# A ring of eight x tiles, fourteen result tiles, and a Pool counter in place of per-slot semaphores

## The chip, the cores and the metric

The kernel runs on one core of a Trainium2 chip. The metric is the device time of one execution in microseconds (us). The engines are TensorE (PE, with its weight loads shown as PEld), VectorE (DVE), ScalarE (ACT), GpSimd (POOL) and SyncE (SP); transfers run on 16 DMA engines that all queues share.

## What is computed

```python
# x: (128, 128, 1024) f32, itok_B_0_7: (128,) int in 0..7, L0_cond_weights: (8, 128, 128) f32
w = weights[subjects]                      # (128, 128, 128): a matrix for each b
out = jnp.einsum('bct,bcd->bdt', x, w)
return x + out
```

For each of 128 batch entries b, a 128 x 128 matrix, one of eight, is chosen by b's subject number, and its transpose is applied to x[b] of 128 x 1024; x itself is added. The kernel adds the identity to the eight matrices once, so that the residual costs nothing afterwards. 67.1 MB are read and 67.1 MB written, all in f32.

## The kernel before

**Tiles and pairs.** A tile is two batch entries, 64 tiles in all; a pair is two tiles, 32 pairs. x is loaded a pair at a time (2.1 MB, 128 partitions, two runs of 8 KB in each), and results are stored a pair at a time (2.1 MB, 16 KB in each partition). Entry a = 0 of a tile lies in the lower 64 partitions, a = 1 in the upper; the 128 rows of c are folded into R = 2 halves.

**Buffers.** `x_ring` has SLOTS = 10 tiles, five pairs; `results` has RESULTS = 6 pairs; `weight_ring` has a picked matrix for each slot of `x_ring`; `product` in PSUM holds PRODUCTS = 2 tiles.

**TensorE** (L233) makes 16 matmuls of 512 columns for a tile. Before each tile it waits until DVE and ACT have emptied the PSUM of two tiles earlier (`dve_copied`, `act_copied`), and before each pair until that pair's x is there. It waits on a semaphore of its slot: `x_first` for the first five pairs, `x_in` later. Its program writes ten tiles out, then a loop of ten tiles that runs five times, then four tiles (L244 to L250). Weights are guarded at a distance: DVE waits for `picked` three tiles ahead before it lets TensorE on (L185, L195).

**DVE and ACT** (L197, L219) copy the products out of PSUM, eight blocks of 32 x 1024 a tile, four or five of them by ACT. Before a pair they wait for the store that last used its place (`pair_out`).

**Pool** goes through the pairs (L137 to L156). For each it waits until the pair five earlier is multiplied, picks four matrices (two copies, L149, for each tile), and issues the load of x into the freed slots (L156). Every second pair it first loads four tiles' subject numbers into registers (L126). The first five loads are SP's (L108), the fifth after the first has landed.

**SP** then issues the 32 stores in order (L118). The store of pair p waits until the pair is copied, and until the load of pair p + 5 has landed:

```python
ahead = pair + PAIR_SLOTS
if ahead < PAIRS - 1:
    sp.wait_ge(x_in[ahead % PAIR_SLOTS], ahead // PAIR_SLOTS * DMA_INC)
```

So loads go ahead of stores; from pair 26 on a store waits for its copies alone.

Of the kernel before, what the change touches and what calls it, by code (L numbers as in the profile page):

```python
# [6 lines left out]
DMA_INC = 16  # L7
SLOTS = 10
PAIR = 2
LOADS_AHEAD = 4  # L10
PRODUCTS = 2
RESULTS = 6
# [3 lines left out]
def subject_residual_kernel(nc, x, subjects, weights, out):  # L16
# [19 lines left out]
    assert LAPS and SLOTS % PRODUCTS == 0 and REST % PRODUCTS == 0  # L36
    PAIRS, PAIR_SLOTS = TILES // PAIR, SLOTS // PAIR
    assert SLOTS % PAIR == 0 and REST % PAIR == 0 and LOADS_AHEAD < PAIR_SLOTS and PAIR * 2 * K == C
# [5 lines left out]
    ACT_BLOCKS = (4, 4, 5, 4, 5)  # L44

# [7 lines left out]
    with ExitStack() as ctx:  # L53
# [27 lines left out]

        picked = ctx.enter_context(nc.semaphore("picked"))
# [19 lines left out]
        def _(sp):  # L102
            sp.dma_start(weight_halves[:, :, :, :],
                         weights.rearrange("(i a) (h r) d -> (a h) i (r d)", a=2, r=R)).then_inc(weights_in, DMA_INC)
            for place in range(PAIR_SLOTS):
                if place >= LOADS_AHEAD:
                    sp.wait_ge(x_first[place - LOADS_AHEAD], DMA_INC)
                sp.dma_start(x_ring[:, place * PAIR:(place + 1) * PAIR, :, :], x_of_pair[place]).then_inc(x_first[place], DMA_INC)  # L108
            for pair in range(PAIRS):
                place = pair % RESULTS  # L110
                sp.wait_ge(act_copied, (pair + 1) * PAIR + PRODUCTS)
                sp.wait_ge(dve_copied, (pair + 1) * PAIR + PRODUCTS)


                ahead = pair + PAIR_SLOTS
                if ahead < PAIRS - 1:
                    sp.wait_ge(x_in[ahead % PAIR_SLOTS], ahead // PAIR_SLOTS * DMA_INC)
                sp.dma_start(out_of_pair[pair], results[:, place, :, :]).then_inc(pair_out[place], DMA_INC)  # L118
# [4 lines left out]
        def _(pool):  # L123
# [9 lines left out]
            for half in (LOW, HIGH):  # L133
                pool.affine_select(eye[half, :], eye[half, :], pattern=[[-1, H]], base=0, channel_multiplier=1,  # L134
                                   compare_op=mybir.AluOpType.not_equal, fill=1.0).then_inc(eye_made, 1)
            pool.wait_ge(clamped, 1)
            for pair in range(PAIRS):  # L137
# [8 lines left out]
                for j in range(PAIR):  # L146
                    slot = pair * PAIR % SLOTS + j
                    for a, half in enumerate((LOW, HIGH)):
                        done = pool.tensor_copy(weight_ring[half, slot, :, :],  # L149
                                                weight_bank[half, bass.ds(numbers[(pair % 2 * PAIR + j) * 2 + a], 1), :, :])  # L150
                    done.then_inc(picked, 1)
                if pair >= PAIR_SLOTS:

                    pool.wait_ge(picked, (pair + 1) * PAIR)
                    place = pair % PAIR_SLOTS
                    pool.dma_start(x_ring[:, place * PAIR:(place + 1) * PAIR, :, :], x_of_pair[pair]).then_inc(x_in[place], DMA_INC)  # L156

        @block.vector
        def _(dve):
# [13 lines left out]
            dve.sem_inc(dve_copied, 1)  # L173
# [11 lines left out]
            dve.wait_ge(picked, PRODUCTS)  # L185
            dve.sem_inc(dve_copied, PRODUCTS - 1)
            for tile in range(TILES):
# [4 lines left out]
                if tile + PRODUCTS < SLOTS:  # L192


                    dve.wait_ge(picked, tile + (PRODUCTS + 1))  # L195
# [27 lines left out]
        def _(pe):  # L223
            def multiply(tile, slot, landed, turns):
                pe.wait_ge(dve_copied, tile + 1)
                pe.wait_ge(act_copied, tile + 1)
                if slot % PAIR == 0:
                    pe.wait_ge(landed[slot // PAIR], turns)
# [14 lines left out]
            pe.wait_ge(picked, 1)  # L243
            for slot in range(SLOTS):  # L244
                multiply(slot, slot, x_first, DMA_INC)
            with pe.Fori(0, LAPS - 1) as lap:
                for slot in range(SLOTS):
                    multiply(lap * SLOTS + SLOTS + slot, slot, x_in, lap * DMA_INC + DMA_INC)
            for slot in range(REST):
                multiply(LAPS * SLOTS + slot, slot, x_in, DMA_INC * LAPS)  # L250
# [14 lines left out]
```

## Time and profile before

| | |
|---|---|
| Median of 3 runs | 324.1 us (323.81 to 324.17) |
| The profiled execution, its own time | 324.13 us |
| Its span, first to last instruction | 322.1 us |
| Busy: PE, DVE, ACT, POOL | 76%, 89%, 89%, 22% |
| DMA engines' mean rate | 419 GB/s |
| Moved, HBM read and written | 67.64 and 67.11 MB |

The span runs from the first instruction to the last; some 2 us of the device time lie around it. Busy shares are averages over the span. The DMA share is the mean busy share of the 16 engines: 1.0 means that none is idle, and it can read a little over 1 because packets overlap. A wait is put down to what ended it.

### The profile page before, as it was taken

Reading aid. Unit: us, or ns where it says so; the run is one execution under the profiler, and the core shown is the slowest. Engines: PE = TensorE matmul, PEld = TensorE weight load, DVE = VectorE, ACT = ScalarE, POOL = GpSimd, SP = SyncE. Lnnn points to the kernel's source line nnn. Section 1 sums busy time; section 2 is a strip of 40 time slices with the busy share of each in tenths; the row PEclk is TensorE's granted clock in tenths of the full one; section 3 lists DMA queues with packets and bytes.
Section 4 is the critical chain, followed back from the end, with each engine's and each line's share of the span. In section 5 each row is a group of like instructions: output and inputs, shape, how many; then the busy total and the mean of one; then the engine's idle time right before and its main releaser. Section 6 shows DMA issues by size and latency. Waiting matters only on the chain.

```text
span 322.1 us, 3197 instructions
## 1 busy us (share of the span) xinstructions
PE 246.1 (76%) x1036; PEld 103.6 (32%) x1036; DVE 286.9 (89%) x238; ACT 285.3 (89%) x283; POOL 71.2 (22%) x162
## 2 busy tenths in 40 slices
PE   8868878888887887789788888878977886885600
PEld 3323333333333333233333333333332333332200
DVE  4399999999999999999999999999999999796730
ACT  4299999999999999999999999999999999894730
POOL 1752222112222222221222222222222200000000
PEclk9999999999999999999999999999999999996955
DMA  7999999999999999999999999999999999999994
GB/s 280 423 423 421 428 441 409 431 424 428 429 426 435 425 432 419 426 441 418 432 435 427 417 430 432 426 422 437 419 429 434 426 430 422 440 426 431 429 429 208
DMA packets 13881, 134.85 MB, mean 419 GB/s; under 512 B 1056, under 2 KB 1584, under 8 KB 1584
## 3 DMA queue, kind: packets, MB, share of 16 engines
q1 hardware_dynamic: 6496, 78.12, 57.2%
q0 software_dynamic: 7344, 56.62, 41.8%
q8 instruction: 3, 0.05, 0.1%
q14 instruction: 6, 0.05, 0.0%
q10 hardware_dynamic: 32, 0.01, 0.0%
HBM read 67.64 MB, written 67.11 MB: 418 GB/s over the span
## 4 chain that ended last, share of the span: by engine, by line
DVE 39%; PE 27%; DMA 13%; ACT 9%; issue 7%; POOL 1%; ACTq 0%; POOLq 0%
DVE results L197 37%; PE product L233 27%; DMA x_ring<-x 11%; ACT results L219 9%; DMA weight_halves<-weights 1%; DVE weight_bank L167 1%; POOL weight_ring L149 1%; ACTq L53 0%; DVE weight_halves L162 0%; POOLq L149 0%; POOLq L126 0%; POOLq L142 0%
## 5 line engine op out<-in xcount | busy, mean ns | idle before, releaser
L219 ACT COPY results<-product 32x1024 f32<-32x1024 f32 x281 | 282.0, 1003 | 19.4 <-PE product L233 14.9
L197 DVE COPY results<-product 32x1024 f32<-32x1024 f32 x231 | 282.2, 1222 | 17.4 <-PE product L233 12.0
L233 PE MATMUL product<-x_ring,weight_ring 64*128 64x512 f32 x1024 | 238.8, 606 | 55.7 <-DVE results L197 39.9
L233 PEld LDWEIGHTS product<-x_ring,weight_ring 64*128 64x128 f32 x1024 | 100.6, 188 | 194.0 <-issue 107.1
L149 POOL COPY weight_ring<-weight_bank 64x256 f32 x128 | 50.9, 398 | 174.8 <-PE product L233 162.6
L156 POOL DMA_DIRECT2D x_ring<-x x27 | 19.4, 720 | 8.0 <-POOL weight_ring L149 8.0
L242 PE MATMUL product<-results 128*128 128x512 f32 x12 | 7.3, 772 | 1.5 <-DVE results L171 1.5
L203 ACT COPY weight_bank<-weight_halves 64x1024 f32<-64x1024 f32 x1 | 2.0, 2039 | 3.1 <-DVE weight_halves L162 3.1
L242 PEld LDWEIGHTS product<-results 128*128 128x128 f32 x12 | 3.0, 257 | 5.0 <-issue 3.5
L167 DVE COPY weight_bank<-weight_halves 64x1024 f32<-64x1024 f32 x3 | 3.2, 1074 | 0.1
L162 DVE TENSOR_TENSOR weight_halves<-weight_halves,eye 128x256 f32<-128x256 f32 x2 | 0.8, 423 | 2.2 <-DMA weight_halves<-weights 2.2
L203 ACT ACT_TABLE_LOAD x1 | 1.3, 1283 | 1.3 <-PEq L257 1.3
L171 DVE MEMSET results<- 128x512 f32 x1 | 0.5, 485 | 0.9 <-PEq L257 0.9
L175 DVE TENSOR_SCALAR subject_row<-subject_row 1x128 int32<-1x128 int32 x1 | 0.2, 215 | 1.0 <-DMA subject_row<-subjects 1.0
L134 POOL TENSOR_SCALAR_AFFINE_SELECT eye<-eye 64x64 f32<-64x64 f32 x2 | 0.5, 235 | 0.3 <-POOL eye L131 0.2
L131 POOL MEMSET eye<- 128x64 f32 x1 | 0.2, 152 | 0.3 <-POOLq L257 0.3
L257 POOL MEMSET const-float32-0.0<- 128x1 f32 x1 | 0.1, 93 | 0.3 <-issue 0.3
L257 POOL MEMSET const-float32-1.0<- 128x1 f32 x1 | 0.1, 93 | 0.0
L257 POOL MEMSET const-bfloat16-1.0<- 128x1 bf16 x1 | 0.1, 93 | 0.0
L257 POOL MEMSET const-uint8-127<- 128x1 uint8 x1 | 0.1, 93 | 0.0
## 6 DMA issues: line engine op xcount, KB each, us to landing
out<-results SPq DMA_DIRECT2D x32, 2048.0 KB, 12.1
x_ring<-x POOLq DMA_DIRECT2D x27, 2048.0 KB, 25.2
x_ring<-x SPq DMA_DIRECT2D x5, 2048.0 KB, 17.4
weight_halves<-weights SPq DMA_DIRECT2D x1, 512.0 KB, 4.1
subject_row<-subjects ACTq DMA_DIRECT2D x1, 8.0 KB, 1.7
```

What stands on the lines that cost most here:

```text
L134: pool.affine_select(eye[half, :], eye[half, :], pattern=[[-1, H]], base=0, channel_multiplier=1, compare_op=mybir.AluOpType.not_equal, fi ...
L149: done = pool.tensor_copy(weight_ring[half, slot, :, :], weight_bank[half, bass.ds(numbers[(pair % 2 * PAIR + j) * 2 + a], 1), :, :])
L156: pool.dma_start(x_ring[:, place * PAIR:(place + 1) * PAIR, :, :], x_of_pair[pair]).then_inc(x_in[place], DMA_INC)
L162: return dve.tensor_tensor(cells, cells, eye[:, :].rearrange("h (s k) -> h s k", s=1).broadcast_to((C, S // 2, H)), add)
L167: return dve.tensor_copy(weight_bank[half, subjects_of, :, :].rearrange("h i r (q k) -> h i r q k", q=Q), weight_halves[source, :, :, :].r ...
L171: dve.memset(results[:, RESULTS - 1, 0, 0:PSUM_BANK_COLS], 0.0).then_inc(zeroed, 1)
L197: last = dve.tensor_copy(target(tile, a, q), rows(tile, a, q))
L203: return act.copy(weight_bank[half, subjects_of, :, :].rearrange("h i r (q k) -> h i r q k", q=Q), weight_halves[source, :, :, :].rearrang ...
L219: last = act.copy(target(tile, a, q), rows(tile, a, q))
L233: last = pe.matmul(product[slot % PRODUCTS][a][:, cols], weight_ring[half, slot, r, :], x_ring[half, slot, r, cols], start=r == 0, stop=r ...
L242: pe.matmul(product[PRODUCTS - 1][0][:, 0:PSUM_BANK_COLS], zeros[:, 0:D], zeros, start=True, stop=True)
L257: nc = bacc.Bacc("TRN2", target_bir_lowering=False, num_devices=1)
```

## The change

The ring of x shrinks from ten tiles to eight (four pairs), and the results grow from six pairs to seven. Eight divides the 64 tiles, so TensorE's program is one loop of eight tiles that runs eight times. A new semaphore `arrived` is counted up by Pool, once for each pair in order, when the pair's weights are picked and its x has landed (`tell`). TensorE waits for this count before each pair, and SP for it before a store. The pair whose load a store waits for is now p + 2 + p // 8, so p + 2 for the first eight pairs and p + 5 for pairs 24 and 25; later pairs wait for none. The four first loads go out without a wait, and DVE no longer stands for the weights.

```diff
-SLOTS = 10
+SLOTS = 8
-LOADS_AHEAD = 4
-RESULTS = 6
+RESULTS = 7
...
+    def load_before(pair):
+        return pair + 2 + pair // 8
...
             for place in range(PAIR_SLOTS):
-                if place >= LOADS_AHEAD:
-                    sp.wait_ge(x_first[place - LOADS_AHEAD], DMA_INC)
                 sp.dma_start(x_ring[...], x_of_pair[place]).then_inc(x_first[place], DMA_INC)
...
-                ahead = pair + PAIR_SLOTS
-                if ahead < PAIRS - 1:
-                    sp.wait_ge(x_in[ahead % PAIR_SLOTS], ahead // PAIR_SLOTS * DMA_INC)
+                if load_before(pair) < PAIRS - 1:
+                    sp.wait_ge(arrived, load_before(pair) + 1)
...
+            def tell(pair):
+                lap, place = divmod(pair, PAIR_SLOTS)
+                pool.wait_ge(picked, (pair + 1) * PAIR)
+                if lap:
+                    pool.wait_ge(x_in[place], lap * DMA_INC)
+                else:
+                    pool.wait_ge(x_first[place], DMA_INC)
+                pool.sem_inc(arrived, 1)
...
+                pick(pair, numbers)
                 if pair >= PAIR_SLOTS:
-                    pool.wait_ge(picked, (pair + 1) * PAIR)
                     place = pair % PAIR_SLOTS
                     pool.dma_start(x_ring[...], x_of_pair[pair]).then_inc(x_in[place], DMA_INC)
+                if pair < 2:
+                    tell(pair)
+                elif pair >= PAIR_SLOTS:
+                    tell(pair - 2)
+            tell(PAIRS - 2)
+            tell(PAIRS - 1)
...
-            dve.sem_inc(dve_copied, 1)
+            dve.sem_inc(dve_copied, PRODUCTS)
...
-            dve.wait_ge(picked, PRODUCTS)
-            dve.sem_inc(dve_copied, PRODUCTS - 1)
...
-                if tile + PRODUCTS < SLOTS:
-                    dve.wait_ge(picked, tile + (PRODUCTS + 1))
...
                 if slot % PAIR == 0:
-                    pe.wait_ge(landed[slot // PAIR], turns)
+                    pe.wait_ge(arrived, pair + 1)
...
-            pe.wait_ge(picked, 1)
-            for slot in range(SLOTS):
-                multiply(slot, slot, x_first, DMA_INC)
-            with pe.Fori(0, LAPS - 1) as lap:
+            with pe.Fori(0, LAPS) as lap:
                 for slot in range(SLOTS):
-                    multiply(lap * SLOTS + SLOTS + slot, slot, x_in, lap * DMA_INC + DMA_INC)
-            for slot in range(REST):
-                multiply(LAPS * SLOTS + slot, slot, x_in, DMA_INC * LAPS)
+                    multiply(lap * SLOTS + slot, slot, lap * PAIR_SLOTS + slot // PAIR)
```

SP's program before, from the first loads on (a row is an instruction with what it waits for; x6 means six alike):

```order
L108 DMA x_ring<-x 128x2x2048 x4
L108 DMA x_ring<-x 128x2x2048 [waits x_first0]
L118 DMA out<-results 128x4096 [waits x_in0,dve_copied,act_copied]
L118 DMA out<-results 128x4096 [waits x_in1,dve_copied,act_copied]
L118 DMA out<-results 128x4096 [waits x_in2,dve_copied,act_copied]
L118 DMA out<-results 128x4096 [waits x_in3,dve_copied,act_copied]
```

SP's whole program now:

```order
L107 UNCONDITIONAL_BRANCH [waits barrier_Pool_Activation_PE_DVE_SP_release]
L109 DMA weight_halves<-weights 128x4x256
L112 DMA x_ring<-x 128x2x2048 x4
L119 DMA out<-results 128x4096 [waits arrived,dve_copied,act_copied] x26
L119 DMA out<-results 128x4096 [waits dve_copied,act_copied] x6
L57 UNCONDITIONAL_BRANCH [waits pair_out4,pair_out3,pair_out5,pair_out2,pair_out6,pair_out1,pair_out0]
```

The fifth load has left SP, and 26 stores wait for Pool's count where each waited for a load's own semaphore.

Pool's program before, the end of the picks of pair 5 and the start of pair 6 (ISA sets a register for the copy behind it):

```order
L149 ISA
L149 COPY weight_ring<-weight_bank 64x256
L156 DMA x_ring<-x 128x2x2048 [waits picked]
L126 TENSOR_LOAD subject_row
L149 ISA [waits multiplied]
```

Pool's program now, the end of the picks of pair 5 and the start of pair 6:

```order
L141 ISA
L141 COPY weight_ring<-weight_bank 64x256
L168 DMA x_ring<-x 128x2x2048
L127 TENSOR_LOAD subject_row [waits picked,x_first3]
L141 ISA [waits multiplied]
```

The wait before the load is gone, and the count of pair 3, with its wait for that pair's x, stands between the load of pair 5 and the register load of pair 6.

TensorE's program before, its start (the warm-up matmuls, then the first tile):

```order
L242 MATMUL product_0<-results 128x512 [waits zeroed]
L242 MATMUL product_0<-results 128x512 x5
L233 MATMUL product_0<-x_ring,weight_ring 128x512 [waits act_copied,x_first0,dve_copied,picked]
L233 MATMUL product_1<-x_ring,weight_ring 128x512
L233 MATMUL product_0<-x_ring,weight_ring 128x512
```

TensorE's program now, its start:

```order
L255 MATMUL product_0<-results 128x512 [waits zeroed]
L255 MATMUL product_0<-results 128x512 x5
L256 UNCONDITIONAL_BRANCH
L256 ISA
L241 ISA [waits act_copied,dve_copied]
L246 MATMUL product_0<-x_ring,weight_ring 128x512 [waits arrived]
L246 MATMUL product_1<-x_ring,weight_ring 128x512
```

The first matmul waited for `picked` and `x_first0`; it waits for Pool's count, inside the loop from the first tile on.

## Rows read from the trace of the kernel before

**Rows 1.** The page: busy share of the DMA engines, 40 equal slices.

```profile
DMA  7999999999999999999999999999999999999994
```

**Rows 2.** Windows: start:end, length, busy (x instructions) by engine, granted clock, DMA.

```profile
core 0: us, PE busy (x) PEld busy (x) DVE busy (x) ACT busy (x) POOL busy (x), PEclk, DMA share, GB/s
0.00:2.00 2.00, 0.54 (x1) 0.50 (x2) 0.48 (x1) 0.72 (x1) 0.82 (x7) 1.00 0.05 17
...
2.00:316.00 314.00, 245.56 (x1036) 103.06 (x1034) 286.43 (x237) 284.56 (x283) 70.37 (x155) 0.97 1.01 427
...
316.00:318.00 2.00, 0.00 (x0) 0.00 (x0) 0.00 (x0) 0.00 (x0) 0.00 (x0) 0.50 0.73 311
318.00:320.00 2.00, 0.00 (x0) 0.00 (x0) 0.00 (x0) 0.00 (x0) 0.00 (x0) 0.50 0.17 74
320.00:322.10 2.10, 0.00 (x0) 0.00 (x0) 0.00 (x0) 0.00 (x0) 0.00 (x0) 0.50 0.02 8
```

**Rows 3.** Timeline of Pool: start us, us, engine, line, operation, idle before and its end.

```profile
9.14 10.71 POOL L149 COPY weight_ring<-weight_bank 64x256 f32 x24 [7.47 <-DVE weight_bank L167]
20.16 0.83 POOL L156 DMA_DIRECT2D x_ring<-x  x1 [0.31 <-POOL weight_ring L149]
27.61 1.73 POOL L149 COPY weight_ring<-weight_bank 64x256 f32 x4 [6.62 <-PE product L233]
29.65 0.72 POOL L156 DMA_DIRECT2D x_ring<-x  x1 [0.31 <-POOL weight_ring L149]
...
254.19 0.72 POOL L156 DMA_DIRECT2D x_ring<-x  x1 [0.30 <-POOL weight_ring L149]
```

**Rows 4.** Waits: who waited for what, us in total, times, longest us.

```profile
SPq L117 <- DMA x_ring<-x: 259.5, 26, 24.7
...
PE product L233 <- DMA x_ring<-x: 3.9, 2, 3.0
```

**Rows 5.** The chain that ended last: start us, us, what.

```profile
0.74 4.07 DMA weight_halves<-weights
...
22.43 1.24 DVE results L197
23.72 3.73 PE product L233 x16
...
272.56 3.72 PE product L233 x16
293.60 6.29 PE product L233 x16
```

**Rows 6.** Timeline of TensorE's first two tiles, and of SP's DMA issues.

```profile
10.03 7.14 PE L233 MATMUL product<-x_ring,weight_ring 64*128 64x512 f32 x32 [1.29 <-POOL weight_ring L149]
...
1.24 8.93 SPq L108 DMA_DIRECT2D x_ring<-x  x5
...
9.80 0.37 SPq L108 DMA_DIRECT2D x_ring<-x  x1
34.98 0.36 SPq L118 DMA_DIRECT2D out<-results  x1
...
294.97 14.43 SPq L118 DMA_DIRECT2D out<-results  x2
...
309.07 0.33 SPq L118 DMA_DIRECT2D out<-results  x1
```

**Rows 7.** Line 126, Pool's register loads: ns min/median/max, first and last start us.

```profile
L126 POOLq TENSOR_LOAD <-subject_row x16: 562/1368/2338, 2.7 to 235.7; - x16
```

**Rows 8.** All loads of x, from issue to landing.

```profile
DMA to landing us min/median/max: 8.5/23.7/39.3
```

**Rows 9.** Windows again: loads alone, loads with stores, stores alone.

```profile
24.00:34.00 10.00, 8.67 (x40) 3.69 (x40) 9.80 (x9) 9.86 (x11) 2.31 (x5) 1.00 1.01 419
...
276.00:284.00 8.00, 6.42 (x32) 2.88 (x30) 7.60 (x7) 7.61 (x8) 0.00 (x0) 1.00 1.02 435
...
294.00:316.00 22.00, 9.30 (x32) 3.78 (x30) 9.46 (x8) 9.03 (x9) 0.00 (x0) 0.66 1.01 432
```

**Rows 10.** The page, DMA queues: one of instruction fetches; packets, MB, share.

```profile
q8 instruction: 3, 0.05, 0.1%
```

## What the change does to the time: the prediction

> **What bounds the kernel now.** I read the whole page first: the 16 DMA engines are busy in every slice but the first and the last two [rows 1]. The windows say it finer: a share of 1.01 and 427 GB/s on average from 2 to 316 us, then 0.73, 0.17 and 0.02 in the last three stretches, so a few engines finish late, while the compute engines, busy for 89% of the span, have nothing left to do there [rows 2]. And the Pool loads, which follow TensorE, are issued from 20.16 to 254.19 us, 26 intervals of 9.00 us [rows 3]. One pair moves 4.19 MB, which at 427 GB/s is 9.82 us. So copying (9.0 us a pair) outruns the transfers (9.8) and the transfers set the end. Third, the waits: SP waits 259.5 us for loads of x before it stores, while TensorE waits only 3.9 us for x in all, 3.0 of it once, before 272.56 [rows 4, 5]. Waits of the compute engines are therefore cheap; what counts is (a) how soon the DMA engines have work, (b) whether they ever run dry, (c) at what rate they run, (d) whether the last store is ready in time, (e) the uneven tail.
>
> **The sum's base.** The profiled execution took 324.13 us, 322.1 of it span; the median of the runs is 324.1, so the sum needs no shift. A measurement of this kernel can tell about 0.2% (0.65 us) from no change.
>
> **Part 1, the start.** SP issues the weights at 0.74 and the first x at 1.24 in both kernels [rows 5, 6]: no change. The first x has landed at 9.80, when SP is released for its fifth load [rows 6]; at 427 GB/s (4.9 us for 2.1 MB) loads 1 to 3 land at 14.7, 19.6 and 24.5. Now there are only these four, and three instructions later in Pool's program matter.
> TensorE no longer starts at Pool's second copy but at Pool's count, after four: copies take 0.45 us each (24 in 10.71 us from 9.14 [rows 3]), so 10.95 plus 0.1, against 10.03 [rows 6]: 1.0 us late. That is compute time, hidden by the 0.8 us a pair by which copying outruns the transfers.
> Pool then stands in the count of pair 1 until 14.7. Only then comes its load of the next subjects into registers, 0.6 to 2.3 us, 1.4 in the median [rows 7], no longer beside copies; then eight copies (a third of 10.71, 3.6 us), to 19.7. Pair 0's products are done at 10.03 + 7.14 + 1.0 = 18.2 [rows 6], so pair 4's picks run at once, 1.73 us, and load 4 goes out at 21.4, between 20.6 and 22.3 (before, load 5 at 20.16 [rows 3]).
> The SP loads feed the engines to about 24 (their landing less the way of the last bytes). From issue to first bytes I have only SP's row: issued at 0.74, and 17 GB/s over 0 to 2 us (34 KB) means a start near 1.9, so 1.2 us; the other end is the whole surplus of that load, 4.07 us less 1.2 us for its data, 2.9 us [rows 2, 5]. From 21.4, load 4 starts between 22.6 and 24.3: a hole of 0 to 0.3 us; I take 0.1. Farther out, if all went slowest, store 0 ends the hole: tile 1's copies end at 23.7 before [rows 5] and 24.7 now, so it starts at 25.9: at most 1.9 us.
> The Trainium skill (DMA: Bandwidth & Descriptors, Specifications) gives first bytes at about 1 us for GpSimd's path and 0.6 for SP's. The row shows 1.2 for SP, twice its figure; with GpSimd's doubled too, load 4 starts at 23.4 and there is no hole. Either way the sum stands within 0.1 us.
> Load 5: pair 1 is multiplied at 27.45 + 1.0; picks and issue as before (27.45 to 29.65, less the 0.3 us wait for the picks, which is gone) give 30.4 [rows 3, 5]. Load 4 and store 0 (4.9 us each) last until 33.9, and it starts by 33.3. From there each 9.0 us brings 9.8 us of work. **Term: +0.1; from 0 to +1.9.**
>
> **Part 2, the long middle.** The ring of x shrinks from five pairs to four. Load p+4 is issued about 2.8 us after pair p is multiplied (picks 1.73, gap 0.3, issue 0.72 [rows 3]) and TensorE wants it three pairs, 27 us, after that moment. Loads took 23.7 us in the median and up to 39.3 [rows 8], so TensorE will wait for x, often, late in the run, at a pace of 9.8 us a pair. Pool is now in front of it: the count of pair q stands between load q+2 and load q+3, and a late x(q) also holds up the picks and load q+3, and SP's store behind the same count. Is anything dry then? When x(q) lands, loads q+1 and q+2 (9.8 us of work) are queued, the count lets a store go, and load q+3 follows 2.8 us later. The margin is 7 us: never dry. Where the rule of the stores steps (pairs 8, 16, 24), a load passes without a store, 4.9 us, still inside it. Seven result places hold what the rule holds back: up to five waiting, one in flight, one being written. **Term: 0.**
>
> **Part 3, the rate.** Loads alone run at 419 GB/s (24 to 34 us), loads with stores at 435, stores alone at 432 [rows 9]. Before, the first store goes out at 34.98 [rows 6]; now at about 24.8, as soon as it is copied, its count (load 2) being there. That takes 10.2 us from the slow rate to the fast one: 10.2 x 16/435 = 0.4 us. The mean of 427 lies half way between 419 and 435, so before some half of the time goes by at the slow rate; each pair's cycle keeps such a stretch (a store of 4.9 us against 9.8), so I count the start only. Bounds: all of it at 435 where 427 was had, 314 x 8/435 = -5.8 us; loads never beside stores, 67.1 MB at 419 and 67.1 at 432, 315.5 us for 314: +1.5. Nearest is the start's own row. **Term: -0.4; I carry -1.5 (a quarter of the slow time gone) to +0.8.**
>
> **Part 4, instructions and the tail.** TensorE's program falls from 24 written-out tiles to 8. Instruction fetches take 0.1% of 16 engines' span on one queue [rows 10], some 5 us of one engine's time. If the lost fetches all sat on the engine that ends last, the end moves by up to about 3 us; spread evenly, by 0.2. TensorE waited for none of it. **Term: -0.1; from -3 to 0.** The added Pool instructions are waits and counts, and its picks and issues fill only 2.8 of each 9.0 us [rows 3].
> The last windows hold about 1.8 us of work for all engines in 6.1 us of time [rows 2]: about 4 us is imbalance. The skill's same page (Latency and other measured facts) says two DMA engines are usually slower beside GpSimd's queue, as a guess at its rings. No row here names an engine. By it one more Pool load (28 for 27) would add 4/27, 0.15 us.
>
> **Part 5, the end.** Let x(30) land at time 0. Then stores 25 to 28 are let go together, 29 to 31 follow, and load 31 is in flight: 5.0 + 7 x 4.9 = 39.3 us of transfers. The last pair needs 15.5 us from its first matmul to the last store's issue (293.60 to 309.07, with one TensorE tile at 6.29 instead of 3.73 [rows 5, 6]), and that store alone some 7.8 us (4.9 plus the 2.9 above). So x(31) may land as late as +16.0. Sharing evenly with one store it lands at +9.9; with two store bytes for each of its own (runs of 16 KB against 8 KB) at +14.7. Hidden, with 1.3 to 6 us to spare. **Term: 0.**
>
> **Sum.** 324.13 + 0.1 + 0 - 0.4 - 0.1 + 0 = **323.7**.
>
> **Rivals.**
> *Faster: the transfers gain rate or the tail evens out.* For it: the early stores are no longer held, and fetches shrink. Against: each pair keeps its stretch of loads alone. Were a quarter of those stretches gone (some 40 of 157 us, x 16/435 = 1.5, in place of the 0.4), the sum is 322.6.
> *Slower: the engines run dry at 24 us*, because load 4 now stands behind the count of pair 1 and Pool's path is slow to start. It decides where load 4's issue and the way to its first byte together pass 24.0: 2.6 us after an issue at 21.4. Price up to 1.9: 323.6 + 1.9 = 325.5. Against it: SP's 1.2 us.
> *Slower at the end:* x(31) later than +16 costs one for one. A load that takes the longest landing seen, 39.3 us, from its issue near -12 lands at +27: +11, 335. For it: four stores start at once against one load. Against: that load before had three loads ahead of it, this one has two.
> *It doesn't do what it says:* the early stores are held as before (SP behind the counts), and nothing moves: 324.1.
>
> **How the numbers follow.** Forecast 0.45, faster rival 0.24, dry start 0.16, late end 0.05, nothing moves 0.10. The range leaves out half of the late end and the outer parts of the others: **321.9 to 325.9**. Around the forecast itself lies 323.1 to 324.4, which gives a third of it to faster (under 323.45), almost none to slower. Faster 0.36, same 0.40, slower 0.24.
>
> **What would show it.** First store issued at 24 to 26 us; the window 24 to 34 near 435 instead of 419; TensorE starts near 11; Pool's first load near 21.4; 28 Pool loads; TensorE's waits for x grow from 3.9 to well over 10 us with the span unchanged; DMA share 1.0 to about 316 us; last store issued between 304 and 312. Wrong if a DMA window before 316 us falls under 0.95, if the last store goes out when the engines are already emptying, or if the share of the last 6 us changes its shape by over 1 us.

## The result and the profile after

The changed kernel takes 325.24 us in the median of 13 runs (324.30 to 326.43), the kernel before 324.04 (323.81 to 324.17): a ratio of 1.0044, interval 1.0032 to 1.0056. It is 1.2 us (0.4%) slower, and the interval leaves no doubt of the direction; 0.4 us faster was forecast. Its 13 runs spread over 2.1 us, the 13 of before over 0.4.

The profiled execution took 325.93 us, 323.8 of it span (before: 324.13 and 322.1), so it is one of the longer ones, and its profile shows the loss larger than a typical run has it. The page's DMA lines, in 40 slices:

```profile
DMA  7999999999999999999999999999999999999995
GB/s 287 423 410 425 316 433 430 419 437 419 438 418 431 436 427 420 436 420 430 435 419 432 428 422 437 422 423 433 424 428 423 438 429 415 437 426 432 431 429 235
```

The busy digits are those of before but for the last [rows 1]. The GB/s line shows what they hide: the fifth slice, 32 to 40 us, moved 316 GB/s, where all others between the first and the last moved 410 to 439. Windows of the changed kernel (columns as in [rows 2]):

```profile
core 0: us, PE busy (x) PEld busy (x) DVE busy (x) ACT busy (x) POOL busy (x), PEclk, DMA share, GB/s
23.00:29.00 6.00, 4.82 (x24) 1.98 (x22) 5.92 (x6) 5.28 (x6) 0.00 (x0) 1.00 1.00 390
34.00:39.00 5.00, 3.98 (x18) 1.46 (x16) 4.86 (x5) 4.93 (x6) 0.00 (x0) 1.00 0.92 272
23.00:39.00 16.00, 13.34 (x60) 5.13 (x56) 15.65 (x14) 15.14 (x16) 2.25 (x5) 1.00 0.99 367
60.00:316.00 256.00, 200.37 (x856) 82.12 (x852) 239.55 (x197) 239.66 (x239) 51.77 (x115) 0.97 1.01 428
316.00:318.00 2.00, 0.00 (x0) 0.00 (x0) 0.00 (x0) 0.00 (x0) 0.00 (x0) 0.50 1.01 434
318.00:320.00 2.00, 0.00 (x0) 0.00 (x0) 0.00 (x0) 0.00 (x0) 0.00 (x0) 0.50 0.82 352
320.00:323.80 3.80, 0.00 (x0) 0.00 (x0) 0.00 (x0) 0.00 (x0) 0.00 (x0) 0.50 0.11 47
```

Before, from the same view:

```profile
34.00:39.00 5.00, 4.32 (x22) 1.85 (x20) 4.88 (x5) 4.93 (x6) 2.21 (x5) 1.00 1.03 428
23.00:39.00 16.00, 13.28 (x58) 5.81 (x60) 15.65 (x14) 15.77 (x17) 4.52 (x10) 1.00 1.02 423
60.00:316.00 256.00, 197.64 (x847) 83.25 (x843) 236.96 (x194) 237.00 (x237) 50.74 (x110) 0.97 1.01 428
```

From 60 us to 316 both kernels move 428 GB/s: the long middle costs nothing. The loss lies ahead of it: 367 GB/s from 23 to 39 us for 423, with 390 in its first six microseconds and 272 from 34 to 39, where the kernel before had 428. The **share** there reads 1.00 and 0.92, so the share alone would not have found the hole: from 35 to 38 us Pool's queue has 117 packets (0.96 MB) at a share of 96.6% of the 16 engines' time, where the kernel before has 153 (1.25 MB) at 100.8%. A packet took longer, and an engine counts as busy meanwhile. The missing bytes, 56 GB/s x 16 us, are 2.1 us at 427. The last windows give some of it back: the 16 engines end closer together (352 GB/s from 318 to 320 us, against 74 in [rows 2]), and the span grows by 1.7 us only.

What stood where, in Pool's timeline, TensorE's, SP's, the chain, and two windows with the granted clock:

```profile
15.60 3.53 POOL L141 COPY weight_ring<-weight_bank 64x256 f32 x8 [2.68 <-DMA x_ring<-x]
20.04 1.74 POOL L141 COPY weight_ring<-weight_bank 64x256 f32 x4 [0.91 <-PE product L246]
21.72 0.83 POOL L168 DMA_DIRECT2D x_ring<-x  x1
30.30 1.73 POOL L141 COPY weight_ring<-weight_bank 64x256 f32 x4 [7.75 <-PE product L246]
31.98 0.72 POOL L168 DMA_DIRECT2D x_ring<-x  x1
...
11.03 8.83 PE L246 MATMUL product<-x_ring,weight_ring 64*128 64x512 f32 x32 [2.70 <-POOLq L153]
...
26.43 17.79 SPq L119 DMA_DIRECT2D out<-results  x3
301.52 9.07 SPq L119 DMA_DIRECT2D out<-results  x2
...
11.03 5.42 PE product L246 x16
...
11.00:17.00 6.00, 5.97 (x20) 2.66 (x22) 0.53 (x1) 0.53 (x1) 2.86 (x8) 0.72 1.00 419
17.00:20.00 3.00, 2.86 (x14) 0.97 (x10) 2.97 (x3) 2.96 (x4) 1.93 (x5) 1.00 1.03 429
```

TensorE idled 2.70 us between the warm-up and the first tile, waiting for Pool's count, and then took 5.42 us for that tile (3.73 before is the usual one [rows 5]). The granted clock had fallen: 0.72 on average from 11 to 17 us (0.50 from 12 to 13, the lower of its two levels, 1.2 GHz), and 1.00 from 17 to 20. Load 4 went out at 21.72, load 5 at 31.98, store 0 at 26.43. Of the three stores in the row from 26.43 on, the second was issued at 35.16; its bytes began only after 39 us, so from 34 to 39 load 5 alone was moving bytes.

TensorE's wait for Pool's count, and the instruction fetches of the page:

```profile
PE product L246 <- POOLq L153: 8.6, 4, 2.8
...
q8 instruction: 1, 0.02, 0.0%
```

TensorE waits for Pool's count 8.6 us in all, the 2.70 before the first tile among them; it waited 3.9 for x before [rows 4].

### The profile page after: what moved, and what is told of

Its sections match the earlier page's. It is cut to its first block, busy times and chain, and to the rows that moved or that the text cites. A ratio compares the mean times of both kernels' runs of the same rounds, so it can differ in the third digit from the quotient of the medians.

```text
span 323.8 us, 3264 instructions
## 1 busy us (share of the span) xinstructions
PE 248.0 (77%) x1036; PEld 101.8 (31%) x1036; DVE 286.9 (89%) x238; ACT 285.2 (88%) x283; POOL 70.3 (22%) x163
## 4 chain that ended last, share of the span: by engine, by line
DMA 46%; DVE 28%; PE 17%; issue 3%; POOL 1%; DVEq 0%; POOLq 0%
DMA x_ring<-x 45%; DVE results L210 26%; PE product L246 17%; POOL weight_ring L141 1%; DMA weight_halves<-weights 1%; DVE weight_bank L186 1%; DVEq L57 0%; DVE weight_halves L181 0%; POOLq L127 0%; POOLq L141 0%; POOLq L153 0%; POOLq L161 0%
## 5 line engine op out<-in xcount | busy, mean ns | idle before, releaser
L232 ACT COPY results<-product 32x1024 f32<-32x1024 f32 x281 | 281.9, 1003 | 19.9 <-PE product L246 16.1
L246 PEld LDWEIGHTS product<-x_ring,weight_ring 64*128 64x128 f32 x1024 | 98.9, 190 | 197.9 <-issue 131.1
L168 POOL DMA_DIRECT2D x_ring<-x x28 | 20.2, 720 | 0.0
```

Of the source, the lines that this page charges most:

```text
L232: last = act.copy(target(tile, a, q), rows(tile, a, q))
L246: last = pe.matmul(product[slot % PRODUCTS][a][:, cols], weight_ring[half, slot, r, :], x_ring[half, slot, r, cols], start=r == 0, stop=r ...
```

## The experiments

Theory 1: the DMA engines get too little work at the start. Why a transfer that is alone in flight then moves fewer bytes I first put down to Pool's path, later to its being alone. Theory 2: four first loads are too few, whatever comes next. Theory 3: Pool's count costs a little with every pair. A table of all, ahead of the single runs; GB/s are from the windows of the profiled execution, the ratio is to the kernel before on the same chip, whose median was 323.84 to 324.04 us.

| kernel | us | ratio, 95% interval | 23 to 39 us | 39 to 60 us | 60 to 316 us |
|---|---|---|---|---|---|
| before | 324.0 | | 423 | 430 | 428 |
| changed | 325.24 | 1.0044 (1.0032, 1.0056) | 367 | 424 | 428 |
| changed, loads 4, 5 by SP | 324.52 | 1.0022 (1.0011, 1.0033) | 424 | 426 | 429 |
| before, ring 8 | 327.18 | 1.0105 (1.0090, 1.0120) | 345 | 415 | 428 |
| changed, 8 warm-ups | 324.86 | 1.0029 (1.0019, 1.0039) | 403 | 428 | 429 |
| changed, count 1 later | 325.14 | 1.0033 (1.0015, 1.0052) | 400 | 427 | 429 |
| before, new rule | 324.18 | 1.0003 (0.9994, 1.0012) | 424 | 428 | 428 |
| before, count | 325.70 | 1.0067 (1.0048, 1.0086) | 411 | 400 | 428 |
| changed, all three repairs | 324.36 | 1.0017 (1.0009, 1.0026) | 423 | 425 | 428 |
| changed, first loads by Pool | 325.12, one run | | 392 | 433 | 428 |
| changed, SP's loads at Pool's hour | 324.91 | 1.0036 (1.0022, 1.0050) | 422 | 429 | 428 |
| before, count and rule | 323.91 | 1.0003 (0.9994, 1.0012) | 426 | 429 | 428 |
| changed, 1 warm-up | 327.14 | 1.0099 (1.0080, 1.0118) | 372 | 411 | 429 |
| before, ring 8, new rule | 324.63 | 1.0015 (1.0006, 1.0024) | 426 | 427 | 428 |
| as SP's at Pool's hour, 8 warm-ups | 324.61 | 1.0019 (1.0010, 1.0028) | 418 | 426 | 429 |

### SP issues loads 4 and 5

```diff
+                if pair < 2:
+                    sp.wait_ge(multiplied, (pair + 1) * PAIR)
+                    sp.dma_start(x_ring[...], x_of_pair[PAIR_SLOTS + pair]).then_inc(x_second[pair], DMA_INC)
                 sp.wait_ge(act_copied, (pair + 1) * PAIR + PRODUCTS)
```

> The changed kernel, with loads 4 and 5 of x issued by SP (waiting for pairs 0 and 1 to be multiplied) instead of Pool. The changed kernel moves only 367 GB/s from 23 to 39 us where the kernel before moves 423; that is 2.1 us of work. Theory 1 (the start runs short because Pool's path is slow to deliver when nothing else is queued): SP can issue load 4 at about 20 and load 5 at 28.8, and its path brings bytes 1.2 us later, so 23 to 39 us comes back to 415 or more and the time to 323.6 to 324.2 us. Theory 2 (four loads at the start are too few, whoever issues the next): the stretch stays below 390 and the time at 325. Theory 3 (the count in front of TensorE and SP costs a little in every pair): the time stays at 325 though the stretch recovers.

```profile
23.00:39.00 16.00, 12.62 (x58) 4.99 (x56) 15.65 (x14) 15.25 (x16) 3.14 (x9) 1.00 1.02 424
...
316.00:318.00 2.00, 0.00 (x0) 0.00 (x0) 0.00 (x0) 0.00 (x0) 0.00 (x0) 0.50 0.75 320
```

The hole is gone (424), and so is its mark on the tail: 320 GB/s from 316 to 318 us, near the 311 of before. The median falls by 0.7 us (the intervals of the two ratios just touch), but stays 0.5 above the kernel before, and above the 323.6 to 324.2 that I expected. SP issued at 18.2 and 28.4 us, 3.5 earlier than Pool, and in this profile the first tile ran on the high clock, so this run alone tells neither path from hour nor the clock's part.

### The ring alone, on the kernel before

```diff
-SLOTS = 10
+SLOTS = 8
-LOADS_AHEAD = 4
+LOADS_AHEAD = 3
-RESULTS = 6
+RESULTS = 7
...
-                if place >= LOADS_AHEAD:
-                    sp.wait_ge(x_first[place - LOADS_AHEAD], DMA_INC)
```

> The kernel before with a ring of eight tiles, seven pairs of results and four first loads without a wait, and nothing else: TensorE waits on the loads' own semaphores, the store of pair p waits for load p + 4. Theory 1 and 2 (the short start): store 0 is held until load 4 has landed, about 30 us, so between 24 and 33 us load 4 is alone and the stretch 23 to 39 us is at least as slow as in the changed kernel, 340 to 370 GB/s; the time is 325 to 327. Theory 3 (the count is to blame): without it the time is the old 324.

```profile
23.00:39.00 16.00, 13.10 (x58) 5.78 (x60) 15.65 (x14) 15.77 (x17) 4.34 (x10) 1.00 0.89 345
```

327.18 us (four runs), the slowest of all, without any count. So the count isn't needed for a loss at the start; whether it costs something with every pair, this run can't tell. SP holds store 0 for load 4, and load 5 goes out at 29.8 us too, so that the engines have next to nothing for two microseconds, and then a store alone:

```profile
28.00:30.00 2.00, 2.00 (x10) 1.04 (x11) 1.99 (x2) 1.98 (x3) 1.55 (x5) 1.00 0.36 147
30.00:35.00 5.00, 3.93 (x20) 1.65 (x18) 4.93 (x5) 4.93 (x6) 0.53 (x1) 1.00 0.88 315
...
29.89 0.36 SPq L116 DMA_DIRECT2D out<-results  x1
```

From 28 to 30 us 147 GB/s are moved, at a share of 0.36, and from 30 to 35, the store alone until load 5's bytes come, 315, at a share of 0.88. This transfer is SP's: a lone one can be slow on SP's queue too.

### More warm-up, and less

```diff
-WARM_UP = 6
+WARM_UP = 8
```

> The changed kernel with eight warm-up matmuls instead of six, so that TensorE doesn't stand idle for 2.7 us before the first tile. Its first tile took 5.42 us instead of 3.73, which makes loads 4 and 5 and stores 0 and 1 late by up to 1.7 us. Theory 1: with the first tile at 3.7 us, load 5 goes out at about 30.3 instead of 31.98, and 23 to 39 us gains half or more of the 2.1 us: 324.2 to 324.7 us. Theory 3: no change, 325.2.

```profile
10.97 7.14 PE L246 MATMUL product<-x_ring,weight_ring 64*128 64x512 f32 x32 [0.71 <-POOLq L153]
23.00:39.00 16.00, 12.62 (x58) 5.00 (x56) 15.65 (x14) 15.27 (x16) 3.81 (x10) 1.00 1.01 403
```

The first two tiles take 7.14 us instead of 8.83, and the stretch comes to 403. Of 1.2 us lost 0.4 come back, less than I expected; the intervals against the kernel before (1.0019 to 1.0039, 1.0032 to 1.0056) overlap, so this gain alone is not shown. With one warm-up the other way:

```diff
-WARM_UP = 6
+WARM_UP = 1
```

> The changed kernel with one warm-up matmul instead of six, so that TensorE's clock is low for its first tiles: the opposite of the run with eight. Theory 1: the first two tiles take up to 7.2 us each, loads 4 and 5 go out 2 to 5 us later, the stretch 23 to 39 us falls below 350, and the time rises to 326 to 328 us. If the start has slack for that, the time stays at 325.2.

```profile
10.97 6.55 PE product L246 x16
23.00:39.00 16.00, 13.49 (x62) 5.53 (x60) 15.72 (x14) 15.13 (x16) 2.85 (x6) 1.00 0.96 372
39.00:60.00 21.00, 16.96 (x76) 6.92 (x74) 20.52 (x18) 20.69 (x22) 6.54 (x15) 1.00 1.00 411
```

The first tile takes 6.55 us after 7.4 us of idling and the time is 327.14. This is the clearest dose: one number for TensorE's warm-up, changed in a kernel that the transfers bound, makes it 1.9 us slower (four runs; the two intervals lie apart). In the profiles the first two tiles end at 20.9 us instead of 19.9. The stretch itself didn't fall below 350, as I had expected (372); the rest of the loss is in the next one (411 for 424).

### Pool's second count, later

```diff
-                if pair < 2:
-                    tell(pair)
+                if pair == 0:
+                    tell(0)
+                elif pair == PAIR_SLOTS - 1:
+                    tell(1)
```

> The changed kernel, but Pool counts pair 1 only after it has picked for pairs 2 and 3, so that it no longer stands in that count until 14.8 us with the picks behind it. Theory 1: load 4 is then bound by pair 0 being multiplied (19.9) and goes out at 21.7 as before, since TensorE's late first tile and not Pool's picks sets it: no change, 325.2, within 0.3. If Pool's standing in the count is what makes load 4 late, it goes out a microsecond earlier and the time falls by 0.5 or more.

No change in the time, as expected (325.14, interval 1.0015 to 1.0052, a wide one), though load 4 went out at 20.3 us in the profile, not at 21.7, and the stretch ran at 400. Its profile had the first tile at 3.73 us after 1.86 us of idling, with the same six warm-ups: whether the first tile finds the high clock varies. So the 400 goes with the clock as much as with the edit; eight warm-ups alone gave 403.

```profile
11.32 7.14 PE L248 MATMUL product<-x_ring,weight_ring 64*128 64x512 f32 x32 [1.86 <-POOLq L153]
```

### The new rule for stores, alone

```diff
-                ahead = pair + PAIR_SLOTS
-                if ahead < PAIRS - 1:
+                ahead = pair + 2 + pair // 8
+                if ahead < PAIR_SLOTS:
+                    sp.wait_ge(x_first[ahead], DMA_INC)
+                elif ahead < PAIRS - 1:
                     sp.wait_ge(x_in[...], ...)
```

> The kernel before with the new rule for stores alone: the store of pair p waits for the load of pair p + 2 + p // 8, on the loads' own semaphores; ring of ten tiles, six pairs of results, five first loads. The first store then goes out at about 23.8 us instead of 34.98. My prediction's step on the rate: 10 us more of loads beside stores, at 435 instead of 419 GB/s, gives 0.4 us back: 323.6. The opposite reading (what is mixed early is missing from the mix later, since loads and stores are fixed amounts, and the runs after the change swing more): 324.0 or above, and the windows from 39 us on no faster than before.

```profile
23.00:39.00 16.00, 13.22 (x58) 5.82 (x60) 15.65 (x14) 15.77 (x17) 4.43 (x10) 1.00 1.02 424
39.00:60.00 21.00, 17.05 (x76) 7.00 (x74) 20.52 (x18) 20.64 (x21) 4.74 (x11) 1.00 1.01 428
60.00:150.00 90.00, 74.26 (x324) 31.04 (x322) 88.15 (x73) 88.39 (x89) 22.92 (x50) 1.00 1.01 429
150.00:270.00 120.00, 95.71 (x410) 41.04 (x408) 113.44 (x93) 113.33 (x114) 27.50 (x60) 0.99 1.01 427
```

324.18 us: no gain. The first store goes out at 23.8 instead of 34.98, and the stretch moves 424 GB/s where it moved 423; the later windows are at 427 to 429. My 0.4 us for the early mix was not there.

### Pool's count alone

```diff
-                    sp.wait_ge(x_in[ahead % PAIR_SLOTS], ahead // PAIR_SLOTS * DMA_INC)
+                    sp.wait_ge(arrived, ahead + 1)
...
-                    pe.wait_ge(landed[slot // PAIR], turns)
+                    pe.wait_ge(arrived, pair + 1)
```

with `tell` in Pool's program as in the change, on the ring of ten.

> The kernel before with Pool's count alone: TensorE and SP wait on it instead of the loads' own semaphores (ring of ten tiles, six pairs of results, old rule, five first loads). Theory 1 (four first loads with nothing behind them): with five, the stretch 23 to 39 us stays at 420 or more and the time at 324.0. Theory 3 (the count costs): up to 325, with no hole in that stretch.

```profile
23.00:39.00 16.00, 12.73 (x58) 5.34 (x56) 15.65 (x14) 15.25 (x16) 4.56 (x10) 1.00 1.00 411
39.00:60.00 21.00, 17.40 (x77) 7.02 (x73) 20.52 (x18) 20.70 (x21) 5.27 (x12) 1.00 1.00 400
```

Neither expectation held: the time is 325.70 (six runs), and the hole is there, but later: from 42 to 45 us, with SP's queue holding nearly all the bytes, 287 GB/s are moved, and from 39 to 60 only 400. The sixth load goes out at 25.8 instead of 20.16 us. A part of that is the count of pair 1, in which Pool stands until 15.56 us, so that its picks end at 22.7 instead of 19.9; for the 3.1 us from there to the issue this trace names no cause. Store 0 waits, now through Pool, until 38.4. From 60 us on it is 428. So the count does cost, but only at the start, through what it makes late.

### All three repairs

The edits of the first run, of the eight warm-ups and of the later count, together:

```diff
-WARM_UP = 6
+WARM_UP = 8
+SP_LOADS = 2
...
-                if pair < 2:
-                    tell(pair)
+                if pair == 0:
+                    tell(0)
+                elif pair == PAIR_SLOTS - 1:
+                    tell(1)
```

> The changed kernel with three repairs: loads 4 and 5 by SP, eight warm-up matmuls, pair 1 counted after the picks for pairs 2 and 3. Theory 1: the start is whole already with SP's loads (324.5 us, 424 GB/s in 23 to 39 us), so the other two add under 0.3 us: 324.2 to 324.6. If what remains of the loss beside the kernel before also comes from the start, it goes to 324.0 or below.

324.36 us, as expected: no better than SP's loads alone within the intervals, and still slower than the kernel before (1.0009 to 1.0026). By the medians the repairs of the start give back 0.9 of the 1.2 us; where the last 0.3 lie is not shown.

### Pool issues the first four loads too

```diff
-            for place in range(PAIR_SLOTS):
-                sp.dma_start(x_ring[...], x_of_pair[place]).then_inc(x_first[place], DMA_INC)
...
+            for place in range(PAIR_SLOTS):
+                pool.dma_start(x_ring[...], x_of_pair[place]).then_inc(x_first[place], DMA_INC)
             pool.memset(eye[:, :], 0.0).then_inc(eye_zero, 1)
```

> The changed kernel with the first four loads of x issued by Pool instead of SP, so that Pool's path is seen with nothing queued before it. Theory 1: in SP's hands the engines run at 423 GB/s from 4 us on; with Pool's, the first microseconds of the first load show the same stretched packets as loads 4 and 5 do in the changed kernel (its 34 to 39 us ran at 272 GB/s), and the first x lands 1 to 3 us later than 9.8. If Pool's path delivers as fast as SP's once started, only the start moves by under a microsecond and 4 to 23 us runs at 423.

```profile
4.00:23.00 19.00, 15.10 (x56) 6.32 (x56) 11.66 (x12) 9.73 (x9) 9.50 (x25) 1.00 1.02 425
23.00:39.00 16.00, 12.60 (x56) 4.88 (x54) 15.65 (x14) 15.13 (x16) 3.36 (x8) 1.00 1.00 392
```

From rest, Pool's path moves 425 GB/s from 4 to 23 us, like SP's. Its first microseconds are not slow; that part of theory 1 falls. The hole stays where it was (392). It is one run, and its time can't be judged.

### SP's loads at Pool's hour, with six and with eight warm-ups

Against the run in which SP issues loads 4 and 5:

```diff
+                    sp.wait_ge(picked, (PAIR_SLOTS + pair + 1) * PAIR)
-                    sp.wait_ge(multiplied, (pair + 1) * PAIR)
```

> The changed kernel with loads 4 and 5 by SP, but no earlier than Pool would issue them: SP waits until Pool has picked for pairs 4 and 5. It tells the path from the hour. SP's loads at 18.2 and 28.4 us had cured the hole (424 GB/s from 23 to 39 us, 324.5 us), Pool's stood at 21.7 and 32.0 (367 GB/s, 325.2 us). If the hour decides (theory 1 in its new form: a transfer that is alone in flight runs slowly, whoever issued it), the stretch stays at 365 to 395 and the time at 325.0 to 325.4. If Pool's path decides, the stretch goes to 415 or more and the time to 324.5.

With six warm-ups the profile had 422 GB/s from 23 to 39 us, SP's loads at 20.8 and 30.2 us, and the first tile on the high clock; the median of five runs is 324.91, between the two expectations and no better than the warm kernel with Pool's loads; the profiled execution was the fastest of the five (324.30). So, with the clock settled:

```diff
-WARM_UP = 6
+WARM_UP = 8
```

> Path against hour once more, with TensorE's first tile surely on the high clock: eight warm-up matmuls, and SP issues loads 4 and 5, but not before Pool has picked for their pairs (20.8 and 30.2 us). The twin with Pool's loads at the same hours gave 403 GB/s from 23 to 39 us and 324.86 us; with six warm-ups and SP's late loads the profile had 422 GB/s. If the path decides: 420 or more and 324.2 to 324.5 us. If the hour decides: about 403 and 324.8.

```profile
33.00:39.00 6.00, 4.61 (x20) 1.97 (x22) 5.84 (x6) 5.92 (x7) 1.46 (x4) 1.00 1.01 412
34.00:38.00 4.00, 3.21 (x16) 1.16 (x12) 3.89 (x4) 3.94 (x5) 0.56 (x2) 1.00 0.99 406
```
```profile
33.00:39.00 6.00, 4.74 (x22) 2.04 (x24) 5.84 (x6) 5.92 (x7) 1.57 (x5) 1.00 0.99 373
34.00:38.00 4.00, 3.13 (x18) 1.13 (x14) 3.89 (x4) 3.94 (x5) 0.67 (x2) 1.00 0.99 354
```

The first fence is SP's late load (issued at 30.4 us), the second Pool's at the same hour (30.2) with the same warm-up: 412 against 373 GB/s. These stretches hold the end of store 0 and the start of store 1 too; from 34 to 37 us, where next to nothing but load 5 moves, it is 412 against 347. The other profiles agree: SP's load 5 moved 410 to 412 in three kernels, Pool's 270 to 347 in four (the changed kernel, eight warm-ups, the later count, first loads by Pool). In the profiles the path decides; in the times it can't be told (324.61 and 324.86, intervals 1.0010 to 1.0028 and 1.0019 to 1.0039). The expected 420 or more was 418, and the time stayed above the 324.2 to 324.5 expected.

That a load is Pool's and alone is not enough, though. The kernel before has such a load at the same hour, the sixth, issued at 29.65 [rows 3]; so has the changed kernel, load 4, from 24 to 28 us:

```profile
34.00:38.00 4.00, 3.32 (x18) 1.40 (x16) 3.89 (x4) 3.94 (x5) 1.51 (x4) 1.00 1.02 420
```

The sixth load of the kernel before moved 420 GB/s, load 4 of the changed kernel 393, and 418 in the kernel with eight warm-ups. What tells these from load 5 (279 over the same 34 to 38 us) no run was made to find. The profiles hint at a head start: over 34 to 37 us, Pool's load issued at 29.65 moved 421, those issued at 30.22, 30.57, 31.09 and 31.98 moved 347, 341, 336 and 270. A rival stands untested beside it: DVE copies for 15.65 of the 16 us from 23 on, and for 11.66 of 19 in the stretch from 4 to 23 us where Pool's path moved 425; no run took DVE's copies away from a late load.

### The count and the rule, on the ring of ten

```diff
-                ahead = pair + PAIR_SLOTS
+                ahead = pair + 2 + pair // 8
                 if ahead < PAIRS - 1:
                     sp.wait_ge(arrived, ahead + 1)
```

> The kernel before (ring of ten, six pairs of results, five first loads) with Pool's count and the new rule for stores. The count alone gave 325.7 us: Pool's sixth load went out at 25.8 instead of 20.2 and the first store at 38.4, and from 39 to 60 us only 400 GB/s were moved. With the new rule the first store goes out at 25, beside two loads. Theory 1: no transfer is alone then, 23 to 60 us runs at 423 or more, and the time is 324.0 to 324.4. If the count itself costs in every pair, the time stays above 325.

```profile
23.00:39.00 16.00, 12.75 (x58) 5.25 (x56) 15.65 (x14) 15.18 (x17) 4.43 (x10) 1.00 1.01 426
39.00:60.00 21.00, 17.48 (x78) 7.10 (x74) 20.52 (x18) 20.65 (x21) 5.35 (x12) 1.00 1.01 429
60.00:316.00 256.00, 196.92 (x848) 81.35 (x848) 238.08 (x195) 237.85 (x238) 49.22 (x110) 0.98 1.01 428
```

323.91 us against 323.84: the whole loss of the count, 1.7 us, is gone as soon as the stores are let go early, though Pool's sixth load is still at 25.9 us. Stores fill the gap that late loads leave. The windows from 60 us on (428) and this time are what rules out theory 3.

### The ring and the rule, without the count

```diff
-SLOTS = 10
+SLOTS = 8
-LOADS_AHEAD = 4
+LOADS_AHEAD = 3
-RESULTS = 6
+RESULTS = 7
...
-                if place >= LOADS_AHEAD:
-                    sp.wait_ge(x_first[place - LOADS_AHEAD], DMA_INC)
...
-                ahead = pair + PAIR_SLOTS
+                ahead = pair + 2 + pair // 8
+                if ahead < PAIR_SLOTS:
+                    sp.wait_ge(x_first[ahead], DMA_INC)
...
```

> The corner that is missing between three parts of the change: ring of eight tiles, seven pairs of results and the new rule for stores, but the loads' own semaphores instead of Pool's count. The kernel before is 324.0, with the new rule 324.2, with the count 325.7, with both 323.9; with the ring of eight alone 327.2, with all three (the changed kernel) 325.2. If four first loads are enough as long as nothing else is late (TensorE starts at 10.1 on a high clock, Pool's load 4 goes out at 19.6 and load 5 at 29.7, store 0 at 23.8), the stretch 23 to 39 us is at 415 or more and the time 324.0 to 324.5: then the change's loss needs the ring and the count together. If four first loads are too few by themselves, the stretch is at 400 or less and the time 324.8 or more.

```profile
23.00:39.00 16.00, 13.23 (x58) 5.81 (x60) 15.65 (x14) 15.77 (x17) 4.46 (x10) 1.00 1.02 426
60.00:316.00 256.00, 197.81 (x848) 83.50 (x844) 237.00 (x194) 236.82 (x237) 53.01 (x115) 0.97 1.01 428
316.00:318.00 2.00, 0.00 (x0) 0.00 (x0) 0.00 (x0) 0.00 (x0) 0.00 (x0) 0.50 0.73 311
```

No hole at all (426), yet 324.63 us, in runs from 324.42 to 324.73. Its spans are 322.3 us in the median, 322.1 for the kernel before in the same rounds; the other 0.4 us lie outside the span. What they are I didn't find. Beside the ring of eight alone it is 2.6 us faster: the rule that gains nothing on the ring of ten is what makes the short ring nearly harmless.

**Together.** By parts, in us: ring of ten 324.0; with rule 324.2; with count 325.7; with both 323.9. Ring of eight 327.2; with rule 324.6; with both 325.2. With the rule, in ratios to the kernel before: count 1.0003, ring 1.0015, both 1.0044; the two together cost more than the sum. (The ring with the count and without the rule was not run.) Theory 1 stands in this form: with stores flowing early the count costs nothing on the ring of ten, and the short ring 0.6 us; with both, loads 4 and 5 are late **and** there are only four loads to live on until then. Theory 2 fails as it was put, since SP's earlier loads, or no count, fill the stretch from the same four. In every kernel the windows from 60 us on are the same, 428 or 429, and theory 3 is out.

## Why the prediction was wrong

**Base and bound.** Right: the transfers set the end, at 428 or 429 GB/s from 60 us to 316 in all 15 kernels.

**Part 1, the start: the step that failed.** The sum had +0.1 us, up to +1.9 in a rival; the experiments give most of the loss to this part (0.9 of 1.2 us come back with the three repairs). Three steps in it were wrong. First, I moved TensorE's first two tiles by the 1.0 us of Pool's count and kept their length of 7.14 us. They took 8.83 in the profile, because the idling before them grew to 2.7 us and the granted clock fell to its lower level. So store 0 went out at 26.43 instead of 24.8, and load 5 at 31.98 instead of 30.4; load 4 was near, 21.72 for 21.4. Second, I asked when each transfer's first byte comes, and took it to run at the full rate from there. Load 5, alone from 34 to 39 us, moved 272 GB/s: at 428 it would have moved the same bytes 1.8 us sooner. Load 4 cost less, with 390 GB/s from 23 to 29 us. Third, I had a store's bytes start 1.2 us after its issue, from SP's first load; store 0, issued at 26.43, moved none before 29 us, which left load 4 alone until then.

The Trainium skill (DMA: Bandwidth & Descriptors, Bandwidth) has smaller transfers slower: it lists 341 GB/s for 1 MB loaded through GpSimd and 425 for 16 MB. The Trainium skill (DMA: Bandwidth & Descriptors, Anatomy of one DMA — SWDGE (gpsimd) path) puts a fixed 2.0 us on each such transfer, beside its bytes at 436 GB/s. By these two figures a load of 2.1 MB alone takes 6.8 us, 308 GB/s (an estimate from that page). That section of the Trainium skill gives most of the 2 us to the confirmation after the last byte, which would not slow a stretch in the middle of a load. Load 5's 272 is nearer to the estimate than to the full rate, but the load alone at 420 in the kernel before is not, nor load 4 at 393: the runs here bear the rule out for one load and not for others. The prediction used the first-byte figure of the Trainium skill and passed these over.

**Part 2, the middle: right.** From 60 us on nothing runs dry. TensorE waits for the count, though less (8.6 us) than the "well over 10" forecast.

**Part 3, the rate: wrong by 0.4 us.** The run with the new rule alone shows no gain (1.0003, 0.9994 to 1.0012). That loads and stores are fixed amounts, so that what is mixed early is unmixed elsewhere, fits it, but is argued and not shown. On the ring of eight the early stores are worth 2.6 us, not through the rate of a mix but because they fill a gap; that was not in the sum.

**Part 4, fetches and tail.** The fetches on the one queue fell from three to one, and the tails of the kernels without a hole (320 and 311 GB/s from 316 to 318 us) are that of before (311 [rows 2]): nothing of the 0.1 us can be seen. The 0.15 us for one more Pool load can't be seen either.

**Part 5, the end: right.** The last store is issued at 310.26 us (the end of the row from 301.52 on, less the issue's own 0.33), inside the 304 to 312 forecast, while the share stays at 1.01 to 318.

**Rivals and signs.** The dry start was the nearest to what came, with a chance of 0.16. It was right in that Pool's late loads after the first four are the place; its deciding point was not. Load 4's bytes came before 24 us (11 packets between 23 and 24), as the forecast had it, and it was load 5, ten microseconds later, that cost most. That its price, 325.5, lies close to the 325.24 measured is luck. Two of the signs set for being wrong came up: the share fell under 0.95 (0.92 from 34 to 39 us), and the last six microseconds changed their shape. The window from 24 to 34 us, which was to be near 435, moved 414.

## What to carry to other kernels

- In a kernel that the transfers bound, work through its first tens of microseconds transfer by transfer, and see that two are in flight; a compute engine's late start can cost time there, whatever slack it has later (one warm-up matmul for six: 1.9 us).
- Read GB/s beside the DMA share: 0.92 to 1.00 of share went with 272 to 390 GB/s.
- A wait that an in-order engine takes on for another delays everything behind it in its program. Here, on the ring of ten, it cost 1.7 us with the stores held back and nothing with the stores let go; on the ring of eight, with the stores let go, the ratio went from 1.0015 to 1.0044.

## What was new about the hardware

- A transfer of 2.1 MB that moves alone sometimes doesn't fill the engines. Load 5 on Pool's path moved 270 GB/s from 34 to 37 us, and 347 in the warm kernel, where SP's load at the same hour moved 412. But Pool's load alone from 34 to 38 us in the kernel before moved 420, and a store of SP's alone 315 (30 to 35 us, ring of eight alone). From rest, with four loads issued in a row, Pool's path moves 425. What decides stays open.
- The first bytes of a store can be late: issued at 26.43 us, none before 29; issued at 35.16, none before 39. In the ring of eight alone, with nothing else moving, a store issued at 29.89 had bytes moving before 31.
- The same six warm-up matmuls don't end at the same time in each profile: after 6.87 us in the changed kernel's, after 8.00 in that of the later count. So the idle stretch before the first tile differs, and with it the clock: after 2.70 us of idling the first tile took 5.42 us, after 1.86 us 3.73, and with the first loads by Pool, after 2.24 us, the two tiles took 7.14 as at the high clock.
- Whether that is behind the spread of the changed kernel's times is not shown. In its 13 runs those with a mean granted clock of 0.971 or more took 324.30 to 325.05 us, those at 0.960 or 0.961 took 325.49 to 326.40; but the slowest, 326.43, had 0.966, and the four runs with one warm-up, whose first tile is slow in the profile, had 0.969 to 0.971 at 326.42 to 327.92. The mean takes in the whole run, and so doesn't tell what the first tile had.
